# A vision tower with a routed layer: moving and reordering steps of the routing tail

## What is computed

```python
input_acts = gelu(jnp.einsum('bsd,nd->bsn', x, input_patterns))
input_acts_seq = input_acts.mean(axis=1)
top_input_acts, top_input_idx = jax.lax.top_k(input_acts_seq, k_input)            # 256 of 2048
input_repr = jnp.zeros((B, n_input), x.dtype).at[brow, top_input_idx].set(top_input_acts)
process_acts = gelu(jnp.einsum('bn,pn->bp', input_repr, process_input_weights))
top_process_acts, top_process_idx = jax.lax.top_k(process_acts, k_process)        # 128 of 1024
process_weights = jax.nn.softmax(top_process_acts, axis=-1)
aggregated_value = jnp.einsum('bk,bkd->bd', process_weights, process_values[top_process_idx])
output_acts_seq = gelu(jnp.einsum('bd,od->bo', aggregated_value, output_input_weights))
top_output_acts, top_output_idx = jax.lax.top_k(output_acts_seq, k_output)        # 256 of 2048
out_per_seq = jnp.einsum('bk,bkm->bm', top_output_acts, output_patterns[top_output_idx])
output = jnp.broadcast_to(out_per_seq[:, None, :], (B, S, d_model))
```

## Time and profile before

| | |
|---|---|
| median of 3 runs | 1633.43 us (1633.07 to 1634.17) |
| profiled execution, its own time | 1632.56 us |
| its span in the trace | 1630.8 us |
| PE, DVE, ACT, POOL busy | 1461.4, 971.0, 940.4, 116.8 us |
| mean granted clock of TensorE | 0.937 of full speed |

### The profile page before, as it was taken

One profiled execution on the slowest core, in us unless ns is written; L12 is line 12 of the kernel. 1 busy time (PEld: TensorE's weight loads), 2 busy tenths in 40 slices (PEclk: granted clock), 3 DMA queues, 4 the chain that ended last, 5 costly groups with the idle time before them and its releaser, 6 DMA issues. The chain is left out here.

```text
span 1630.8 us, 31726 instructions
## 1 busy us (share of the span) xinstructions
PE 1461.4 (90%) x9685; PEld 1369.6 (84%) x9685; DVE 971.0 (60%) x2429; ACT 940.4 (58%) x3348; POOL 116.8 (7%) x243
## 2 busy tenths in 40 slices
PE   5899999999999999999999999999999998764321
PEld 4799999999999999999999999999999998661220
DVE  6766655555555555555555555555565543585686
ACT  4566666666666666666666666666666654761440
POOL 0000000000000000000000000000000000000000
PEclk9999999999999999999999999999999999757555
DMA  9311111111111111111111111111110000376007
GB/s 202 81 45 45 45 44 44 44 41 41 40 43 44 44 44 44 44 44 44 44 42 40 39 40 39 40 40 40 40 40 10 10 11 11 105 245 263 0 0 315
DMA packets 53092, 99.35 MB, mean 61 GB/s; under 512 B 16704, under 2 KB 35648, under 8 KB 52032
## 3 DMA queue, kind: packets, MB, share of 16 engines
q1 hardware_dynamic: 50768, 96.91, 20.4%
q10 hardware_dynamic: 2288, 2.00, 0.6%
HBM read 73.17 MB, written 25.69 MB: 61 GB/s over the span
## 5 line engine op out<-in xcount | busy, mean ns | idle before, releaser
L625 ACT ACTIVATE ffn<-ffn 128x196 f32<-128x196 f32 x1024 | 329.0, 321 | 208.4 <-PE ffn L513 207.9
L513 PE MATMUL ffn<-x_t_hi,pat_w_hi 128*128 128x392 f32 x1024 | 361.7, 353 | 1.7 <-DVE x_t_lo L780 1.7
L513 PE MATMUL ffn<-x_t_lo,pat_w_hi 128*128 128x392 f32 x1024 | 348.5, 340 | 0.0
L513 PE MATMUL ffn<-x_t_hi,pat_w_lo 128*128 128x392 f32 x1024 | 348.4, 340 | 0.0
L716 DVE SCALAR_TENSOR_TENSOR shared<-shared,gen 98x512 f32<-98x512 f32 x64 | 44.0, 688 | 278.4 <-ACT shared L598 278.4
L513 PEld LDWEIGHTS ffn<-x_t_hi,pat_w_hi 128*128 128x128 f32 x1024 | 192.9, 188 | 6.1 <-DVE x_t_lo L780 2.0
L513 PEld LDWEIGHTS ffn<-x_t_lo,pat_w_hi 128*128 128x128 f32 x1024 | 194.3, 190 | 1.2
L625 ACT ACTIVATION_READ_ACCUMULATOR ffn<-ffn 128x1 f32 x1024 | 193.1, 189 | 0.0
L513 PEld LDWEIGHTS ffn<-x_t_hi,pat_w_lo 128*128 128x128 f32 x1024 | 193.0, 189 | 0.0
L443 PE MATMUL gen<-qkvu_w_hi,h_t_hi 128*98 128x512 f32 (+1 forms) x512 | 172.4, 337 | 2.4 <-ACT q_t L580 2.1
L443 PE MATMUL gen<-qkvu_w_lo,h_t_hi 128*98 128x512 f32 (+1 forms) x512 | 172.5, 337 | 0.0
(11 more groups left out here) (209 smaller groups left out, 2743.1 us busy)
## 6 DMA issues: line engine op xcount, KB each, us to landing
raw<-in_x_dram SPq DMA_DIRECT2D x752, 56.0 KB, 2.0
h_dram<-h SPq DMA_DIRECT2D x128, 98.0 KB
process_nat<-ocess_input_weights_dram SPq DMA_DIRECT2D x8, 1024.0 KB, 4.8
process_t<-h_dram SPq DMA_DIRECT2D x8, 896.0 KB, 12.0
out_dram<-process_t SPq DMA_DIRECT2D x8, 896.0 KB, 6.7
h_early<-h_dram SPq DMA_DIRECT2D x4, 896.0 KB, 12.7
out_dram<-h_early SPq DMA_DIRECT2D x4, 896.0 KB, 4.0
pat_nat<-_ffn_input_patterns_dram SPq DMA_DIRECT2D x1, 2048.0 KB, 15.8
```

What stands on the lines that cost most here:

```text
L513: last = pe.matmul(fb[f % FFN_BANKS][:, 0:T2], a[:, d, f * P:(f + 1) * P], b[:, d, :], start=n == 0, stop=n == 3 * s.halves - 1)
L625: last = act.activation(cols, cols, ACT.Gelu, accum_out=gelu_sum[:, par, at:at + 1])
```

## The change

All of it is in `route`.

- *Low words*: ScalarE copies the low words (`keep_low_words`, behind its first round of a wide stage) in place of DVE's L1293.
- *Larger counts*: in the wide stages DVE no longer counts the numbers above the found one. ScalarE sums signs against the found one less a half (`count_tie_signs`, behind the last round and, in stage 1, behind the last table copy); `place_ties` turns these into the quota by two products with matrices made for it, so that one quota operation is left. The narrow stage keeps both counts, but PE adds its two products in PSUM.
- *Selection per half*: L1302 is split into two halves of 512, each followed by its L1305.
- *Values product turned*: `values` is the stationary operand and the 64 columns of weights move, so that the result comes out turned; the column of ones, the scaling copy, the transpose and its copy go. DVE sums the weights, PE adds the halves, DVE inverts, and the inverse becomes the scale of the GELU of L1219.
- *GELU table early*: a one-column GELU (`spare`) stands behind the exponential.
- *Identity products*: `keep_busy(n)` puts n products of the 128 x 128 identity with itself ahead of `place_ties` and ahead of the transposes. In stage 1 PE waits for the last table copies before these.
- *First store*: the first chunk of 7 tokens is added and stored as 2 and 5.

```diff
@@ gpsimd
-            pool.memset(values[:, :, s.d_pv:], 1.0).then_inc(masks_made, 1)
+            pool.tensor_tensor(tie_share[:], other_half[:], same_image[:], ALU.subtract).then_inc(masks_made, 1)
@@ tensor
+            def keep_busy(products):
+                for _ in range(products):
+                    pe.matmul(prod[3][:, 0:P], w.ident[:], w.ident[:], start=True, stop=True)
+
             def place_ties(stage):
                 pe.wait_ge(ties_counted, stage)
-                pe.matmul(sums[:, 3:4], other_half[:], n_ties[:], start=True, stop=True)
-                pe.matmul(sums[:, 4:5], same_image[:], n_sure[:], start=True, stop=True).then_inc(ties_placed, 1)
+                if stage == 2:
+                    pe.matmul(sums[:, 6:7], other_half[:], n_ties[:], start=True, stop=False)
+                    pe.matmul(sums[:, 6:7], same_image[:], n_sure[:], start=False, stop=True).then_inc(ties_placed, 1)
+                else:
+                    pe.wait_ge(signs_counted, stage + 1)
+                    pe.matmul(sums[:, 6:8], image_minus_half[:], tie_signs[:], start=True, stop=False)
+                    pe.matmul(sums[:, 6:8], image_ties[:], wide_ties[:], start=False, stop=True).then_inc(ties_placed, 1)
...
+            pe.wait_ge(copied, fills)
+            keep_busy(3)
             place_ties(1)
-            pe.wait_ge(copied, fills)
+            keep_busy(4)
             turn_chosen(wide, 2, 0)
...
+            pe.wait_ge(copied, fills + out_fills)
+            keep_busy(5)
             place_ties(2)
+            keep_busy(5)
             turn_chosen(narrow, 1, 2)
-            pe.wait_ge(copied, fills + out_fills)
-            chosen_product([prod[2][0:B, 0:s.d_pv + 1]], PROC_T, lambda t, v: values[:, t, :], 2).then_inc(product, 1)
-            pe.wait_ge(result, 2)
-            pe.transpose(turn[1][:, 0:B], small[:], w.ident[0:B, 0:B]).then_inc(chosen_turned, 1)
+            pe.wait_ge(chosen_kept, 3)
+            for t in range(PROC_T):
+                u, at = divmod(t, PROC_T // 2)
+                last = pe.matmul(prod[2][:, 0:B], values[:, t, :], chosen_t[:, at * P + u * B:at * P + (u + 1) * B],
+                                 start=t == 0, stop=t == PROC_T - 1)
+            last.then_inc(product, 1)
+            pe.wait_ge(weights_summed, 1)
+            pe.matmul(prod[3][:, 0:1], same_image[:], weight_sum[:], start=True, stop=True).then_inc(weights_summed, 1)
             pe.wait_ge(chosen_kept, 4)
...
+            pe.wait_ge(wide_made, 2)
+            keep_busy(6)
             place_ties(3)
+            keep_busy(4)
             turn_chosen(wide, 2, 3)
@@ scalar
+            def keep_low_words(stage):
+                act.wait_ge(keys_made, stage)
+                act.activation(low_word[:], sure[:].bitcast(I16).rearrange("p (n w) -> p n w", w=2)[:, :, 0],
+                               ACT.Copy).then_inc(low_word_made, 1)
+
+            def count_tie_signs(search):
+                act.wait_ge(tried_made, (search + 1) * (ROUNDS + 1))
+                act.activation(below[:], tried[:, 0:1], ACT.Copy, bias=-0.5).then_inc(signs_counted, 1)
+                act.wait_ge(signs_counted, search)
+                with nc.allow_low_precision(reason="whole numbers up to 1024"):
+                    act.activation(reached_too[:, 0:HALF], ties[:], ACT.Sign, scale=-1.0, bias=below[:],
+                                   accum_out=tie_signs[:, 0:1]).then_inc(signs_counted, 1)
...
+            act.activation(image_ties[:], tie_share[:], ACT.Copy)
...
+            act.activation(wide_ties[:], blank[:, 0:2], ACT.Copy)
+            act.activation(tie_signs[:], blank[:, 0:2], ACT.Copy)
...
+            act.activation(spare[:], peak[:], ACT.Gelu)
             keep_chosen(1, 2)
+            act.wait_ge(product, 2)
+            act.activation(small_t[:], prod[2][:, 0:B], ACT.Copy).then_inc(chosen_kept, 1)
             act.wait_ge(softmax, 3)
-            act.activation(small[:], prod[2][0:B, 0:s.d_pv], ACT.Copy, scale=total[:]).then_inc(result, 1)
-            act.wait_ge(chosen_turned, 4)
-            act.activation(small_t[:], turn[1][:, 0:B], ACT.Copy).then_inc(chosen_kept, 1)
             for n in range(2):
                 act.wait_ge(output_product, n + 1)
-                last = act.activation(wide[:, n * 512:(n + 1) * 512], prod[n][:], ACT.Gelu)
+                last = act.activation(wide[:, n * 512:(n + 1) * 512], prod[n][:], ACT.Gelu, scale=total[:])
@@ vector, count_ties
-                after(tie_step, dve.tensor_scalar(is_tie, src, kth, 0.0, ALU.is_gt, ALU.add, accum_out=n_sure[:]))
+                if number == 2:
+                    after(tie_step, dve.tensor_scalar(is_tie, src, kth, 0.0, ALU.is_gt, ALU.add, accum_out=n_sure[:]))
...
-                after(tie_step, dve.tensor_scalar(quota[:], sums[:, 4:5], -1.0, float(k), ALU.mult, ALU.add))
-                after(tie_step, dve.tensor_tensor(quota[:], quota[:], sums[:, 3:4], ALU.subtract))
+                left_over = k if number == 2 else k - src.shape[1]
+                after(tie_step, dve.tensor_scalar(quota[:], sums[:, 6:7], -1.0, float(left_over), ALU.mult, ALU.add))
@@ vector, wide_top_k
-                dve.tensor_copy(low_word[:], words[:, :, 0])
...
+                dve.wait_ge(low_word_made, stage)
...
-                after(tie_step, dve.scalar_tensor_tensor(ties[:], chosen_t[:], quota[:], ties[:], ALU.is_le, ALU.add))
                 for n in range(2):
                     cols = slice(n * 512, (n + 1) * 512)
+                    after(tie_step, dve.scalar_tensor_tensor(ties[:, cols], chosen_t[:, cols], quota[:], ties[:, cols],
+                                                             ALU.is_le, ALU.add))
                     dve.scalar_tensor_tensor(wide[:, cols], ties[:, cols], tried[:, 0:1], wide[:, cols],
                                              ALU.is_gt, ALU.mult).then_inc(chosen, 1)
...
-            dve.wait_ge(product, 2)
-            dve.reciprocal(total[:], prod[2][0:B, s.d_pv:s.d_pv + 1]).then_inc(softmax, 1)
+            dve.wait_ge(chosen, 3)
+            dve.reduce_sum(weight_sum[:], narrow[:], axis=AX.X).then_inc(weights_summed, 1)
+            dve.wait_ge(weights_summed, 2)
+            dve.reciprocal(total[:], prod[3][:, 0:1]).then_inc(softmax, 1)
...
+        FIRST_TOKENS = 2
+        pieces = [(0, slice(0, FIRST_TOKENS * D)), (0, slice(FIRST_TOKENS * D, CHUNK * D))]
+        pieces += [(g, slice(0, CHUNK * D)) for g in range(1, CHUNKS)]
```

More of the change, by code:

```diff
@@ L891, in route @@
         process_t = sb("process_t", [P, IN_T, s.n_proc])
-        values = sb("values", [P, PROC_T, s.d_pv + 1])
+        values = sb("values", [P, PROC_T, s.d_pv])
         output_nat = sb("output_nat", [P, OUT_T, s.d_pv])
@@ L932, in route @@
         peak = sb("peak", [P, 1])
-        total = sb("total", [B, 1])
+        spare = sb("spare", [P, 1])
+        total = sb("total", [P, 1])
+        weight_sum = sb("weight_sum", [P, 1])
         kth = sb("kth", [P, 1])
-        small = sb("small", [B, s.d_pv])
         small_t = sb("small_t", [P, B])
@@ L954, in route @@
         n_sure = sb("n_sure", [P, 1])
+        tie_share = sb("tie_share", [P, P])
+        image_ties = sb("image_ties", [P, P], F32R)
+        wide_ties = sb("wide_ties", [P, 2], F32R)
+        tie_signs = sb("tie_signs", [P, 2], F32R)
+        below = sb("below", [P, 1])
         turn = [ctx.enter_context(nc.psum_tensor(f"rt{b}", [P, 512], F32)) for b in range(3)]
@@ L1012, in _ @@
                 sp.dma_start(homes[n][:, at], rows(h2_dram, g)).then_inc(h2_in[n], 16)
[L1013 to L1016, removed]
+            for n, (g, words) in enumerate(pieces):
+                home, at = h2_home(g)
+                sp.wait_ge(added, n + 1)
+                sp.dma_start(rows(out, g)[:, words], homes[home][:, at, words]).then_inc(out_stored[n % 4], 16)
             for n in range(4):
-                sp.wait_ge(out_stored[n], 16 * len(range(n, CHUNKS, 4)))
+                sp.wait_ge(out_stored[n], 16 * len(range(n, len(pieces), 4)))
         @block.gpsimd
@@ L1147, in _ @@
             last.then_inc(product, 1)
-            pe.wait_ge(result, 4)
+            pe.wait_ge(result, 2)
             pe.wait_ge(routed_low, 1)
@@ L1188, in _ @@
                 count_too(n, n // ROUNDS)
+                if n == 0:
+                    keep_low_words(1)
                 if n >= 1:
@@ L1198, in keep_chosen @@
                     act.activation(chosen_t[:, n * 512:(n + 1) * 512], turn[n][:], ACT.Copy).then_inc(chosen_kept, 1)
+            count_tie_signs(1)
             keep_chosen(2, 0)
@@ L1223, in _ @@
                     count_too(search * ROUNDS + n, search)
-            keep_chosen(2, 4)
+                    if search == 2 and n == 0:
+                        keep_low_words(2)
+            count_tie_signs(3)
+            keep_chosen(2, 3)
             act.wait_ge(product, 3)
-            act.activation(routed[0][:], prod[2][:, 0:D], ACT.Copy).then_inc(result, 2)
```

(9 more changed lines are left out.)

17 lines of the change are left out of this document (9 added, 8 removed).

## The result

The kernel after takes 1628.47 us in the median of 7 runs (1627.07 to 1630.28), the kernel before 1634.16 beside it (7 runs, 1633.07 to 1636.79): a ratio of 0.9966, interval 0.9957 to 0.9975, so 5.7 us less, where 9.0 less was forecast. The forecast of 1624.4 was 4 us too low. The time is close to that of rival B, 1627.8, the sum without the clock. In part that is luck: the clock did not stay away. In the profile it gave in stages 1 and 3 and took in stage 2, and the three come to -0.70 only.

A forecast was written before the change was run, and what follows sets the result against it. The prediction took the tail (1400 to 1631 us) as one chain of waits between engines. Its terms summed to -5.6 us without the clock and -9.0 with it, from 1633.43 to 1624.4 us; range 1621.5 to 1629.5.

The forecast's parts named there:

- rival B: Stages' products: identity products do not raise the clock; 1627.8 us, or 1629.5 if stage 2's output product slows too; chance 0.28.
- the sum without the clock: Tail: all savings except those from a higher PE clock, together -5.6 us, giving 1627.8 us.
- the clock: PE in three stages: identity products bring 2.4 GHz earlier; -3.4 us, from stage 2 whole and stage 3's product.
- change the shape of a product: Stage 2's values product turned: -0.8 us on the path to the output product, -0.2 on the product itself.
- a store that starts earlier: Final add and store loop: a smaller first piece starts the DMA drain sooner; -0.55 us, bounds -1.4 and +0.1.
- an operation that is "hidden" on POOL: Setup ahead of round 0: a POOL subtraction replaces a memset; claimed to cost zero.
- Loads of 128 columns: Stage 2's turned values product: 16 instructions at 0.22 us, 3.5 in all, so -0.2, bounds -1.8 and +0.3.

The follow-up runs named there:

- e3: Kernel after plus three identity products in each of the 15 rounds of stage 2's rank search: 1627.59 us, ratio to before 0.9963.
- e5: e3 with nine and ten identity products instead of five and five in stage 2, and two behind its transposes: 1625.97 us, ratio to before 0.9953.
- e6: e5 plus five identity products in each of stage 3's last four search rounds, and nine and nine instead of six and four behind them: 1623.25 us, ratio 0.9935.

## What to carry to other kernels

Work that is put into a wait to keep a clock up has to fill the wait at the durations of the high clock; sized at the low clock, it leaves half of the wait empty once it succeeds (e3 against e5). Before you change the shape of a product, look at which clock its successor lives on. And a store that starts earlier, or an operation that is "hidden" on POOL, is only worth what the next arrival, or the neighbour on DVE, leaves of it.

## What was not expected

- The clock: four rounds with identity products between the sums, PE busy for 11.54 of 12 us, left it at 0.50 (e6), while stage 1's 14 instructions with eight transposes behind them raised it in each of ten profiles. What counts is not settled here.
- A wait that had long been met: in stage 3 DVE waits for the low words (`low_word_made`), which ScalarE had copied by 1530.15, some 22 us earlier. The row of the kernel after:

```profile
1552.26 0.75 DVE L1353 TENSOR_SCALAR sure<-word,tried 128x1024 f32<-128x1024 int16 x1 [0.23 <-DVE tried L1314]
```

DVE idles 0.23 ahead of L1353, which starts 3.29 after the last round's count began, where it was 3.08 before. The same wait in stage 1 costs nothing (3.09 there, before and after). That the wait is the cause was not tried.
- Loads of 128 columns (3.48 us for 16 in the turned product, 0.218 each) and of 64 (3.30 for 16) differ by 5%.
